# Heads of an attention: five of eight high parts on ScalarE, and scaling and splitting of sums in instructions of 1024 columns

## The chip, the cores and the metric

The kernel runs on one core of one Trainium2 chip. The time is device microseconds of one execution, the median of three runs where runs are compared, and one further execution carries the profile. The core's engines are TensorE (PE), VectorE (DVE), ScalarE (ACT), GpSimd (POOL) and SyncE (SP); a DMA is issued from the queue of SP or POOL here.

## The reference, cut

Six layers follow one another, each added to x of 4 x 1024 x 128 after a layer norm: experts, the attention of heads, experts, a recurrent layer, a second attention, a recurrent layer. The change is in the attention of heads alone:

```python
def _L0_attn_ref(x, weight):
    b, t, c = x.shape                 # 4, 1024, 128
    nh = NUM_HEADS                    # 16
    hs = c // nh                      # 8
    y = x.reshape(b, t, nh, hs).transpose(0, 2, 1, 3)
    scores = jnp.einsum('bhtk,bhsk->bhts', y, y) / math.sqrt(hs)
    attn = jax.nn.softmax(scores, axis=-1)
    o = jnp.einsum('bhts,bsc->bhtc', attn, x)
    o = o.transpose(0, 2, 1, 3).reshape(b, t, nh * c)
    return o @ weight
```

So there are 64 heads (4 batches of 16), each with scores of 1024 x 1024, a softmax over them, a product with the batch's 1024 x 128 values, and a product with 128 rows of the weight.

## The kernel before, in words

The function `head_attention` walks over 64 heads one after another. A head's scores are cut in eight tiles of 128 x 1024. Scores are symmetric but for the softmax's division, so the exponentials' row sums are kept apart and the division is done later, on the sums over the values: `scale` holds the inverse sums, spread over the partitions by a trip through DRAM.

A float32 product is made of three products of a reduced type (fp32r): each operand is split in a high part, which is a copy into fp32r, and a low part, which is the operand less its high part (`product`, lines 88 to 90). The steps for tile s of head h, whose running number is n = 8h + s:

- PE, `scores` (line 783): tiles s and s + 1 together, for even s, once the exponentials of all earlier tiles are done; two pairs of PSUM banks.
- ACT (line 835): the exponential of the tile out of PSUM into one of four buffers `e`, with the row sums; it waits for the scores and for the low part of tile n - 4.
- High part `e_hi`: on ACT (line 842) for the tiles in `ACT_HIGH`, directly behind that tile's exponential; on DVE (line 893) for the others.
- DVE (line 895): low part `e_lo`, which waits for the high part; DVE takes the tiles in order.
- PE, `weighted_rows`: the product of the tile with the values, six matmuls of 512 columns (two halves of 1024), six tiles behind the scores.

Once per head come the steps on its sums, here called u. DVE `scale_sums(h - 1)` (line 861) stands behind the low part of tile 5 of head h: it multiplies the sums of head h - 1, in two PSUM banks, by `scale`. The two banks are taken over by `weighted_rows` of tile 0 of head h, which waits for the scaling, for each half apart. ACT `u_highs(h - 1)` (line 825) stands behind the copy of tile 7, DVE `u_lows(h - 1)` (line 867) behind the low part of tile 7. PE `add_head(h - 2)` stands in the step of tiles 6 and 7, ahead of `weighted_rows` of tiles 0 and 1, and multiplies u by the weight. After 16 heads DVE's `add_batch` adds the finished batch to x, behind the low part of tile 3.

The order on each engine is that of the program; semaphores tie the engines. The order on PE in the steps of two tiles is:

```python
                for n in range(0, COUNT * TILES + TRAIL, 2):
                    if n < COUNT * TILES:
                        scores(n // TILES, n % TILES)
                    if n >= TRAIL:
                        if n % TILES == TRAIL and n // TILES >= 2:
                            add_head(n // TILES - 2)
                        for m in (n - TRAIL, n - TRAIL + 1):
                            weighted_rows(m // TILES, m % TILES)
```

SP stores the inverse sums and loads `scale` and the right operand of the scores, POOL loads the left operand; both run up to two heads ahead.

Of the kernel before, what the change touches and what calls it, by code (L numbers as in the profile page):

```python
# [8 lines left out]
F32R = mybir.dt.float32r  # L9
# [7 lines left out]
P = 128  # L17
BATCH, T = 4, 1024
TOKENS = BATCH * T
BANK = 512  # L20
# [53 lines left out]
def f(ap):  # L74

    return ap.bitcast(F32)
# [587 lines left out]
def head_attention(nc, tag, psum, consts, dram, x):  # L664


    with ExitStack() as ctx:
# [20 lines left out]
        inverse = sb(f"{tag}_inverse", [P, 2, 32])  # L688
        inverse_rows = sb(f"{tag}_inverse_rows", [P, 2, 32])
        scale = sb(f"{tag}_scale", [P, 2, T])  # L690
        u = sb(f"{tag}_u", [P, HALVES, BANK])
        u_hi, u_lo = sb(f"{tag}_u_hi", [P, 2, HALVES, BANK], F32R), sb(f"{tag}_u_lo", [P, 2, HALVES, BANK], F32R)
        SCORES, OUT, SUM = 0, 4, 6

        left_loaded, right_loaded = ([sem(f"{side}_{parity}") for parity in ("even", "odd")] for side in ("left", "right"))
# [6 lines left out]
        out_done, scaled_ready, u_high, u_low = sem("out"), sem("scaled"), sem("u_high"), sem("u_low")  # L702
        sum_done, added = sem("sum_done"), sem("added")
        HEAD_LOADS = 8
        ACT_HIGH = (1, 3, 5, 7)
        TRAIL = 6
        COUNT = BATCH * HEADS
        VALUE_BANKS = TOKENS // BANK
# [23 lines left out]
        with nc.Block() as block:  # L732
            @block.sync
            def _(sp):
                load_head(sp, right, (0, 1), 0, right_loaded)
                load_head(sp, right, (0, 1), 1, right_loaded)
                for h in range(COUNT):
                    sp.wait_ge(inverse_ready, h + 1)
                    after(sp, scale_loaded[h % 2], 16 * (h // 2))
                    for b in range(P // 32):  # L740
                        sp.dma_start(inverse_dram[h % 2, :].rearrange("(s b i) -> b s i", b=P // 32, i=32)[b],
                                     inverse_rows[b * 32:b * 32 + TILES, h % 2, :]).then_inc(inverse_stored, 16)
                    sp.wait_ge(inverse_stored, 16 * (P // 32) * (h + 1))
                    after(sp, scaled_ready, (h - 1) * HALVES)
                    sp.dma_start(scale[:, h % 2, :], inverse_dram[h % 2:h % 2 + 1, :].to_broadcast([P, T])
                                 ).then_inc(scale_loaded[h % 2], 16)
                    if h + 2 < COUNT:
                        sp.wait_ge(scores_done, (h + 1) * TILES)
                        load_head(sp, right, (0, 1), h + 2, right_loaded)
# [9 lines left out]
            @block.tensor  # L759
            def _(pe):  # L760
                def add_head(g):

                    cols = slice(g % HEADS * P, (g % HEADS + 1) * P)
                    pe.wait_ge(u_low, (g + 1) * HALVES)
                    if g % HEADS == 0:
                        after(pe, added, g // HEADS * HALVES)
                    for half in range(HALVES):
                        last = product(pe, psum[:, SUM + half, :], (w_hi[:, cols], w_lo[:, cols]),
                                       (u_hi[:, g % 2, half, :], u_lo[:, g % 2, half, :]),
                                       first=g % HEADS == 0, last=g % HEADS == HEADS - 1)  # L770
                    last.then_inc(sum_done, 1)

                def scores(h, s):

                    if s == 0:
                        pe.wait_ge(left_loaded[h % 2], 16 * HEAD_LOADS * (h // 2 + 1))
                        pe.wait_ge(right_loaded[h % 2], 16 * HEAD_LOADS * (h // 2 + 1))
                    after(pe, exp_done, h * TILES + s)
                    for tile in (s, s + 1):
                        for half in range(HALVES):  # L780
                            g = 2 * (tile % 2) + half
                            rows = slice(32 * g, 32 * (g + 1))
                            last = pe.matmul(psum[:, SCORES + g, :], left[rows, h % 2, tile * P:(tile + 1) * P],  # L783
                                             right[rows, h % 2, half * BANK:(half + 1) * BANK], start=True, stop=True)
                        last.then_inc(scores_done, 1)

                def weighted_rows(h, s):
                    pe.wait_ge(low, h * TILES + s + 1)
                    at_v = slice(h // HEADS * T + s * P, h // HEADS * T + (s + 1) * P)
                    for half in range(HALVES):  # L790
                        at = slice(half * BANK, (half + 1) * BANK)
                        if s == 0:
                            after(pe, scaled_ready, (h - 1) * HALVES + half + 1)
                        last = product(pe, psum[:, OUT + half, :], (v_hi[:, at_v], v_lo[:, at_v]),
                                       (e_hi[:, s, at], e_lo[:, s, at]), first=s == 0, last=s == TILES - 1)
                    last.then_inc(out_done, 1)

                for k in range(2 * VALUE_BANKS):
                    if k >= 8:
                        pe.wait_ge((v_by_act, v_by_dve)[k % 2], (k - 8) // 2 + 1)  # L800
                    for q in range(BANK // P):
                        at = slice(k % VALUE_BANKS * BANK + q * P, k % VALUE_BANKS * BANK + (q + 1) * P)
                        last = pe.transpose(psum[:, k % 8, q * P:(q + 1) * P],
                                            f((row_hi, row_lo)[k // VALUE_BANKS][:, at]), consts["identity"])
                    last.then_inc(turned, 1)
                pe.wait_ge(v_by_act, VALUE_BANKS)
                pe.wait_ge(v_by_dve, VALUE_BANKS)
# [8 lines that stand above are left out]
                for g in (COUNT - 2, COUNT - 1):  # L816
                    add_head(g)

            @block.scalar
            def _(act):  # L820
                def u_highs(g):
                    after(act, sum_done, g - 1)
                    for half in range(HALVES):
                        act.wait_ge(scaled_ready, g * HALVES + half + 1)
                        act.copy(u_hi[:, g % 2, half, :], u[:, half, :]).then_inc(u_high, 1)

                for k in range(0, 2 * VALUE_BANKS, 2):
                    act.wait_ge(turned, k + 1)
                    act.copy(turned_value(k), psum[:, k % 8, :]).then_inc(v_by_act, 1)
                for n in range(COUNT * TILES):  # L830
                    h, s = n // TILES, n % TILES
                    act.wait_ge(scores_done, n + 1)
                    after(act, low, n - 3)
                    wide = psum[:, SCORES + 2 * (s % 2):SCORES + 2 * (s % 2) + 2, :].rearrange("p a b -> p (a b)")
                    act.activation(e[:, s % 4, :], wide, ACT.Exp, scale=HEAD ** -0.5,  # L835
                                   accum_out=sums[:, h % 2, s:s + 1]).then_inc(exp_done, 1)
                    if s in ACT_HIGH:
                        act.wait_ge(exp_done, n + 1)
                        after(act, out_done, n - (TILES - 1))
                        if n < BATCH:  # L840
                            act.wait_ge(copied[n], BATCH_COPIED)
                        act.copy(e_hi[:, s, :], e[:, s % 4, :]).then_inc(act_high, 1)  # L842
                    if s == TILES - 1 and h >= 1:
                        u_highs(h - 1)
                u_highs(COUNT - 1)

            @block.vector
            def _(dve):
# [7 lines left out]
                def scale_sums(g):  # L856
                    dve.wait_ge(scale_loaded[g % 2], 16 * (g // 2 + 1))
                    dve.wait_ge(out_done, (g + 1) * TILES)
                    for half in range(HALVES):
                        after(dve, u_low, (g - 1) * HALVES + half + 1)  # L860
                        dve.tensor_tensor(u[:, half, :], scale[:, g % 2, half * BANK:(half + 1) * BANK],  # L861
                                          psum[:, OUT + half, :], ALU.mult).then_inc(scaled_ready, 1)

                def u_lows(g):
                    for half in range(HALVES):
                        dve.wait_ge(u_high, g * HALVES + half + 1)
                        dve.tensor_tensor(u_lo[:, g % 2, half, :], u[:, half, :], f(u_hi[:, g % 2, half, :]),
                                          ALU.subtract).then_inc(u_low, 1)

                def add_batch(b):  # L870
                    dve.wait_ge(sum_done, (b + 1) * HEADS)
# [864 lines left out]
```

## Time and profile before

| what | us |
|---|---|
| median of three runs (2739.37 to 2742.69) | 2742.0 |
| the profiled execution's own time | 2743.51 |
| its span, first to last instruction | 2741.4 |
| PE busy (93% of the span) | 2545.0 |
| DVE busy (81%) | 2223.1 |
| ACT busy (66%) | 1821.2 |
| POOL busy (45%) | 1231.3 |

All times in the rows are in microseconds from the span's start, except means of one instruction, in nanoseconds. The heads' first scaling stands at 682.5 and their last at 1657.5. In the timeline a row with x2 or x4 is a run of that many instructions and its length is from the first start to the last end; successive instructions of an engine overlap a little, so steps are best read from start to start. A bracket behind a row is the engine's idle time ahead of it and the instruction that released it. PE's matmuls are pipelined: they are shown 0.39 long, but follow one another after 0.23 at full clock.

### The profile page before, as it was taken

The numbers are of one execution on the slowest core, as the hardware profiler recorded it, in microseconds if no ns is written. First come the engines' busy times: TensorE is split into PE (matmuls) and PEld (weight loads), VectorE is DVE, ScalarE is ACT, GpSimd is POOL, SyncE is SP. The second block draws the span as 40 slices with busy tenths as digits, with TensorE's granted clock in tenths as the row PEclk, the third lists the DMA queues.
The fourth block names the chain that finished last, engine by engine and source line by source line (L and its number), as shares of the span: only waits on it lengthen the run. The fifth ranks groups of instructions, "written<-read, shape, count | busy, mean of one in ns | idle before, by whom it ended". The sixth has DMA issues, their size and how long they took to land. (4 is left out here: it accounts for less than half of the span.)

```text
span 2741.4 us, 35099 instructions
## 1 busy us (share of the span) xinstructions
PE 2545.0 (93%) x11075; PEld 1905.2 (69%) x11075; DVE 2223.1 (81%) x3277; ACT 1821.2 (66%) x3026; POOL 1231.3 (45%) x1265
## 2 busy tenths in 40 slices
PE   6899999996999999999999997899999998788778
PEld 3688888874666666666666664688888885476556
DVE  6778777776999999999999996777787775567655
ACT  3455555556888888888888884455555555557665
POOL 3466666664323232332323322466666662245401
PEclk9999999998999999999999999999999999888999
DMA  3566666644333333333333321566666640100000
GB/s 85 118 138 145 145 142 135 136 103 164 98 107 99 106 102 97 109 100 104 104 103 101 98 93 34 127 144 138 135 146 145 143 105 8 32 16 8 8 8 31
DMA packets 107385, 271.47 MB, mean 99 GB/s; under 512 B 30784, under 2 KB 35648, under 8 KB 107072
## 3 DMA queue, kind: packets, MB, share of 16 engines
q1 hardware_dynamic: 82192, 235.42, 34.7%
q0 software_dynamic: 24576, 33.62, 4.4%
q8 instruction: 88, 1.44, 0.2%
q14 instruction: 97, 0.79, 0.1%
q10 hardware_dynamic: 432, 0.20, 0.0%
HBM read 258.35 MB, written 10.76 MB: 98 GB/s over the span
## 5 line engine op out<-in xcount | busy, mean ns | idle before, releaser
L614 POOL TENSOR_TENSOR moe_experts_lo<-moe_experts_hidden,moe_experts_hi 128x512 fp32r<-128x512 f32 x512 | 661.1, 1291 | 340.6 <-ACT moe_experts_hi L552 340.4
L895 DVE TENSOR_TENSOR heads_e_lo<-heads_e,heads_e_hi 128x1024 fp32r<-128x1024 f32 x512 | 616.1, 1224 | 25.7
L559 ACT ACTIVATE psum<-psum 128x512 f32<-128x512 f32 x512 | 298.0, 582 | 479.8 <-PE psum L90 479.8
L729 POOL DMA_DIRECT2D heads_left<-heads_parts x512 | 306.5, 612 | 671.3 <-PE psum L783 610.7
L835 ACT ACTIVATE heads_e<-psum 128x1024 f32<-128x1024 f32 x512 | 520.0, 1023 | 108.2 <-PE psum L783 108.2
L586 DVE TENSOR_TENSOR moe_experts_weighted<-moe_spread,psum 128x512 f32<-128x512 f32 x512 | 350.8, 685 | 190.2 <-PE psum L90 186.4
L88 PE MATMUL psum<-heads_e_hi,heads_v_lo 128*128 128x512 f32 x1024 | 429.4, 419 | 18.0 <-DVE heads_u L861 18.0
L88 PE MATMUL psum<-moe_n_hi,moe_w_lo 128*128 128x512 f32 x1024 | 400.8, 391 | 4.2 <-PEq L54 3.9
L89 PE MATMUL psum<-heads_e_lo,heads_v_hi 128*128 128x512 f32 x1024 | 404.2, 395 | 0.0
L90 PE MATMUL psum<-heads_e_hi,heads_v_hi 128*128 128x512 f32 x1024 | 400.9, 391 | 0.0
L89 PE MATMUL psum<-moe_n_lo,moe_w_hi 128*128 128x512 f32 x1024 | 400.2, 391 | 0.0
L90 PE MATMUL psum<-moe_n_hi,moe_w_hi 128*128 128x512 f32 x1024 | 399.8, 390 | 0.0
L591 DVE TENSOR_TENSOR moe_experts_hidden<-moe_experts_weighted,psum 128x512 f32<-128x512 f32 x512 | 351.9, 687 | 34.4 <-POOL moe_experts_lo L614 17.7
L552 ACT CAST moe_experts_hi<-moe_experts_hidden 128x512 fp32r<-128x512 f32 x512 | 313.4, 612 | 1.3 <-DVE moe_experts_hidden L591 1.3
L88 PEld LDWEIGHTS psum<-heads_e_hi,heads_v_lo 128*128 128x128 f32 x1024 | 192.6, 188 | 124.3 <-issue 67.7
L842 ACT CAST heads_e_hi<-heads_e 128x1024 fp32r<-128x1024 f32 x256 | 269.3, 1052 | 8.1
L88 PEld LDWEIGHTS psum<-moe_n_hi,moe_w_lo 128*128 128x128 f32 x1024 | 193.3, 189 | 46.7 <-POOLq L624 5.4
L90 PEld LDWEIGHTS psum<-heads_e_hi,heads_v_hi 128*128 128x128 f32 x1024 | 193.2, 189 | 45.3
L90 PEld LDWEIGHTS psum<-moe_n_hi,moe_w_hi 128*128 128x128 f32 x1024 | 193.3, 189 | 40.5
L89 PEld LDWEIGHTS psum<-moe_n_lo,moe_w_hi 128*128 128x128 f32 x1024 | 193.4, 189 | 40.0
L89 PEld LDWEIGHTS psum<-heads_e_lo,heads_v_hi 128*128 128x128 f32 x1024 | 193.2, 189 | 32.3
L88 PE MATMUL psum<-moe_experts_hi,moe_w_lo 128*128 128x512 f32 x512 | 199.8, 390 | 2.4 <-POOL moe_experts_lo L614 2.4
(403 smaller groups left out, 4093.8 us busy)
## 6 DMA issues: line engine op xcount, KB each, us to landing
moe_spread<-moe_mask SPq DMA_DIRECT2D x128, 1024.0 KB, 9.8
heads_right<-heads_parts SPq DMA_DIRECT2D x512, 64.0 KB
heads_left<-heads_parts POOLq DMA_DIRECT2D x512, 64.0 KB, 2.5
heads_scale<-heads_inverse_copy SPq DMA_DIRECT2D x64, 512.0 KB, 3.7
moe_experts_raw<-in_gate SPq DMA_DIRECT2D x16, 256.0 KB, 11.7
moe_experts_raw<-in_up SPq DMA_DIRECT2D x16, 256.0 KB, 11.8
moe_experts_raw<-in_down SPq DMA_DIRECT2D x16, 256.0 KB, 11.6
heads_parts<-heads_e_hi SPq DMA_DIRECT2D x16, 256.0 KB, 3.2
```

What stands on the lines that cost most here:

```text
L88: pe.matmul(out, w_lo, x_hi, start=first, stop=False, skip_group_check=True)
L89: pe.matmul(out, w_hi, x_lo, start=False, stop=False, skip_group_check=True)
L90: return pe.matmul(out, w_hi, x_hi, start=False, stop=last, skip_group_check=True)
L552: act.copy(hi[:, p, :], hidden[:, p % 2, :]).then_inc(high_ready, 1)
L559: act.activation(psum[:, GATE + p % 2, :], psum[:, GATE + p % 2, :], ACT.Silu).then_inc(silu_ready, 1)
L586: dve.tensor_tensor(weighted[:, p % 2, :], spread[:, pair % 2, p, j * BANK:(j + 1) * BANK], psum[:, UP + p % 2, :], ALU.mult).then_inc(wei ...
L591: dve.tensor_tensor(hidden[:, p % 2, :], weighted[:, p % 2, :], psum[:, GATE + p % 2, :], ALU.mult).then_inc(hidden_ready, 1)
L614: pool.tensor_tensor(lo[:, p, :], hidden[:, p % 2, :], f(hi[:, p, :]), ALU.subtract).then_inc(low_ready, 1)
L729: eng.dma_start(f(tile[row:row + 2 * HEAD, h % 2, :]), parts_dram[dims, order:order + 2, at]).then_inc(loaded[h % 2], 16)
L835: act.activation(e[:, s % 4, :], wide, ACT.Exp, scale=HEAD ** -0.5, accum_out=sums[:, h % 2, s:s + 1]).then_inc(exp_done, 1)
L842: act.copy(e_hi[:, s, :], e[:, s % 4, :]).then_inc(act_high, 1)
L895: dve.tensor_tensor(e_lo[:, s, :], e[:, s % 4, :], f(e_hi[:, s, :]), ALU.subtract).then_inc(low, 1)
```

## The change

Tile 4 joins the tiles whose high part ACT makes, so ACT makes five and DVE three. The sums are held as 1024 columns in one piece: the scaling on DVE, the high part on ACT and the low part on DVE are one instruction of 1024 columns each, where they were two of 512. The semaphores of these steps count heads and no longer halves, so PE waits for the whole scaling ahead of both halves of `weighted_rows` of tile 0.

```diff
-        u = sb(f"{tag}_u", [P, HALVES, BANK])
-        u_hi, u_lo = sb(f"{tag}_u_hi", [P, 2, HALVES, BANK], F32R), sb(f"{tag}_u_lo", [P, 2, HALVES, BANK], F32R)
+        u = sb(f"{tag}_u", [P, T])
+        u_hi, u_lo = sb(f"{tag}_u_hi", [P, 2, T], F32R), sb(f"{tag}_u_lo", [P, 2, T], F32R)
...
-        ACT_HIGH = (1, 3, 5, 7)
+        ACT_HIGH = (1, 3, 4, 5, 7)
...
-                    after(sp, scaled_ready, (h - 1) * HALVES)
+                    after(sp, scaled_ready, h - 1)
...
-                    pe.wait_ge(u_low, (g + 1) * HALVES)
+                    pe.wait_ge(u_low, g + 1)
...
-                            after(pe, scaled_ready, (h - 1) * HALVES + half + 1)
+                            after(pe, scaled_ready, h)
...
                     after(act, sum_done, g - 1)
-                    for half in range(HALVES):
-                        act.wait_ge(scaled_ready, g * HALVES + half + 1)
-                        act.copy(u_hi[:, g % 2, half, :], u[:, half, :]).then_inc(u_high, 1)
+                    act.wait_ge(scaled_ready, g + 1)
+                    act.copy(u_hi[:, g % 2, :], u[:, :]).then_inc(u_high, 1)
...
-                    for half in range(HALVES):
-                        after(dve, u_low, (g - 1) * HALVES + half + 1)
-                        dve.tensor_tensor(u[:, half, :], scale[:, g % 2, half * BANK:(half + 1) * BANK],
-                                          psum[:, OUT + half, :], ALU.mult).then_inc(scaled_ready, 1)
+                    after(dve, u_low, g)
+                    dve.tensor_tensor(u[:, :], scale[:, g % 2, :], psum[:, OUT:OUT + 2, :].rearrange("p a b -> p (a b)"),
+                                      ALU.mult).then_inc(scaled_ready, 1)
 
                 def u_lows(g):
-                    for half in range(HALVES):
-                        dve.wait_ge(u_high, g * HALVES + half + 1)
-                        dve.tensor_tensor(u_lo[:, g % 2, half, :], u[:, half, :], f(u_hi[:, g % 2, half, :]),
-                                          ALU.subtract).then_inc(u_low, 1)
+                    dve.wait_ge(u_high, g + 1)
+                    dve.tensor_tensor(u_lo[:, g % 2, :], u[:, :], f(u_hi[:, g % 2, :]), ALU.subtract).then_inc(u_low, 1)
```

The order of ACT's instructions in one head of the steady part, from behind the high sums of one head to those of the next, before (x2 is two exponentials in a row):

```order
L825 CAST heads_u_hi<-heads_u 128x512 x2
L835 ACTIVATE heads_e,heads_sums<-psum 128x1024 x2
L842 CAST heads_e_hi<-heads_e 128x1024
L835 ACTIVATE heads_e,heads_sums<-psum 128x1024 x2
L842 CAST heads_e_hi<-heads_e 128x1024
L835 ACTIVATE heads_e,heads_sums<-psum 128x1024 x2
L842 CAST heads_e_hi<-heads_e 128x1024
L835 ACTIVATE heads_e,heads_sums<-psum 128x1024 x2
L842 CAST heads_e_hi<-heads_e 128x1024
```

and ACT's same head after the change:

```order
L825 CAST heads_u_hi<-heads_u 128x1024
L835 ACTIVATE heads_e,heads_sums<-psum 128x1024 x2
L842 CAST heads_e_hi<-heads_e 128x1024
L835 ACTIVATE heads_e,heads_sums<-psum 128x1024 x2
L842 CAST heads_e_hi<-heads_e 128x1024
L835 ACTIVATE heads_e,heads_sums<-psum 128x1024
L842 CAST heads_e_hi<-heads_e 128x1024
L835 ACTIVATE heads_e,heads_sums<-psum 128x1024
L842 CAST heads_e_hi<-heads_e 128x1024
L835 ACTIVATE heads_e,heads_sums<-psum 128x1024 x2
L842 CAST heads_e_hi<-heads_e 128x1024
```

The copy of tile 4 now stands between the exponentials of tiles 4 and 5. On DVE the same head, from behind the transposed inverse sums to the low part of the sums, before:

```order
L893 CAST heads_e_hi<-heads_e 128x1024
L895 TENSOR_TENSOR heads_e_lo<-heads_e,heads_e_hi 128x1024 x2
L893 CAST heads_e_hi<-heads_e 128x1024
L895 TENSOR_TENSOR heads_e_lo<-heads_e,heads_e_hi 128x1024 x2
L893 CAST heads_e_hi<-heads_e 128x1024
L895 TENSOR_TENSOR heads_e_lo<-heads_e,heads_e_hi 128x1024 x2
L861 TENSOR_TENSOR heads_u<-heads_scale,psum 128x512 x2
L893 CAST heads_e_hi<-heads_e 128x1024
L895 TENSOR_TENSOR heads_e_lo<-heads_e,heads_e_hi 128x1024 x2
```

and after the change (line numbers of the changed kernel):

```order
L890 CAST heads_e_hi<-heads_e 128x1024
L892 TENSOR_TENSOR heads_e_lo<-heads_e,heads_e_hi 128x1024 x2
L890 CAST heads_e_hi<-heads_e 128x1024
L892 TENSOR_TENSOR heads_e_lo<-heads_e,heads_e_hi 128x1024 x4
L860 TENSOR_TENSOR heads_u<-heads_scale,psum 128x1024
L890 CAST heads_e_hi<-heads_e 128x1024
L892 TENSOR_TENSOR heads_e_lo<-heads_e,heads_e_hi 128x1024 x2
```

DVE's copy of tile 4 is gone, so the low parts of tiles 2 to 5 stand in a row, and the scaling behind them is one instruction. PE's, SP's and POOL's instructions keep their order.

## Rows read from the trace of the kernel before

**Rows 1.** Windows: busy us (instructions) of each engine, granted PE clock, DMA share, GB/s.
```profile
720.00:1600.00 880.00, 864.95 (x3975) 596.53 (x3974) 849.49 (x1029) 779.62 (x1252) 271.03 (x452) 1.00 0.34 103
...
683.60:687.00 3.40, 3.40 (x9) 2.65 (x8) 3.37 (x5) 2.12 (x4) 3.05 (x5) 0.51 0.38 104
```
**Rows 2.** Timeline of PE, one head: start, length, line, operation [idle before <-releaser].
```profile
1112.82 0.50 PE L783 MATMUL psum<-heads_right,heads_left 32*128 32x512 f32 x4
...
1117.95 0.40 PE L90 MATMUL psum<-heads_u_hi,heads_w_hi 128*128 128x512 f32 x1
1118.56 0.47 PE L88 MATMUL psum<-heads_e_hi,heads_v_lo 128*128 128x512 f32 x1 [0.22 <-DVE heads_u L861]
...
1128.30 0.50 PE L783 MATMUL psum<-heads_right,heads_left 32*128 32x512 f32 x4
```
**Rows 3.** Timeline of ACT, the same head.
```profile
1113.36 1.03 ACT L835 ACTIVATE heads_e<-psum 128x1024 f32<-128x1024 f32 x1 [0.19 <-PE psum L783]
...
1114.37 1.02 ACT L835 ACTIVATE heads_e<-psum 128x1024 f32<-128x1024 f32 x1
...
1115.51 1.05 ACT L842 CAST heads_e_hi<-heads_e 128x1024 fp32r<-128x1024 f32 x1
...
1118.93 1.05 ACT L842 CAST heads_e_hi<-heads_e 128x1024 fp32r<-128x1024 f32 x1
1119.89 1.13 ACT L825 CAST heads_u_hi<-heads_u 128x512 fp32r<-128x512 f32 x2
```
**Rows 4.** Timeline of DVE, the same head.
```profile
1114.51 0.69 DVE L893 CAST heads_e_hi<-heads_e 128x1024 fp32r<-128x1024 f32 x1
1115.23 1.23 DVE L895 TENSOR_TENSOR heads_e_lo<-heads_e,heads_e_hi 128x1024 fp32r<-128x1024 f32 x1
1116.59 1.23 DVE L895 TENSOR_TENSOR heads_e_lo<-heads_e,heads_e_hi 128x1024 fp32r<-128x1024 f32 x1
1117.73 0.68 DVE L861 TENSOR_TENSOR heads_u<-heads_scale,psum 128x512 f32<-128x512 f32 x1
...
1118.93 0.69 DVE L893 CAST heads_e_hi<-heads_e 128x1024 fp32r<-128x1024 f32 x1
```
**Rows 5.** The scaling's line 861: who waited for it (us in all, times).
```profile
  PE psum L88: 18.0, 63
```
**Rows 6.** Groups by line and shape, 680 to 1660: busy us, mean ns | idle before.
```profile
L895 DVE TENSOR_TENSOR heads_e_lo<-heads_e,heads_e_hi 128x1024 fp32r<-128x1024 f32 x500 | 601.4, 1224 | 25.1
...
L867 DVE TENSOR_TENSOR heads_u_lo<-heads_u,heads_u_hi 128x512 fp32r<-128x512 f32 x128 | 82.3, 684 | 0.1
```
**Rows 7.** Timeline of DVE, a head in which a finished batch is added.
```profile
931.38 1.28 DVE L861 TENSOR_TENSOR heads_u<-heads_scale,psum 128x512 f32<-128x512 f32 x2
...
943.45 1.28 DVE L874 TENSOR_TENSOR x<-x,psum 128x512 f32<-128x512 f32 x2
...
947.65 1.28 DVE L861 TENSOR_TENSOR heads_u<-heads_scale,psum 128x512 f32<-128x512 f32 x2
```
**Rows 8.** Timelines of PE and DVE, from the first head to the second.
```profile
682.47 1.28 DVE L861 TENSOR_TENSOR heads_u<-heads_scale,psum 128x512 f32<-128x512 f32 x2
...
683.30 0.55 PE L88 MATMUL psum<-heads_e_hi,heads_v_lo 128*128 128x512 f32 x1 [1.81 <-DVE heads_u L861]
683.64 0.63 PE L89 MATMUL psum<-heads_e_lo,heads_v_hi 128*128 128x512 f32 x1
684.07 0.63 PE L90 MATMUL psum<-heads_e_hi,heads_v_hi 128*128 128x512 f32 x1
...
699.49 1.28 DVE L861 TENSOR_TENSOR heads_u<-heads_scale,psum 128x512 f32<-128x512 f32 x2
```
**Rows 9.** Timeline behind the last head.
```profile
1656.94 1.28 DVE L861 TENSOR_TENSOR heads_u<-heads_scale,psum 128x512 f32<-128x512 f32 x2 [6.22 <-PE psum L90]
...
1659.71 0.51 PE L88 MATMUL psum<-heads_u_hi,heads_w_lo 128*128 128x512 f32 x1 [1.48 <-DVE heads_u_lo L867]
```
**Rows 10.** The page's DMA issues: KB each, us to landing.
```profile
heads_scale<-heads_inverse_copy SPq DMA_DIRECT2D x64, 512.0 KB, 3.7
```

More of the change, by code:

```diff
@@ L767, in add_head @@
                     for half in range(HALVES):
+                        at = slice(half * BANK, (half + 1) * BANK)
                         last = product(pe, psum[:, SUM + half, :], (w_hi[:, cols], w_lo[:, cols]),
-                                       (u_hi[:, g % 2, half, :], u_lo[:, g % 2, half, :]),
+                                       (u_hi[:, g % 2, at], u_lo[:, g % 2, at]),
                                        first=g % HEADS == 0, last=g % HEADS == HEADS - 1)
```

## The prediction

> **What bounds the kernel now.** I read the windows by stage first [rows 1]. The change touches only the heads of the first attention, some 980 of 2741 us. In its steady part (720 to 1600 us) PE is busy 864.95 of 880 us, VectorE (DVE) 849.49 and ScalarE (ACT) 779.62, PE at a granted clock of 1.00. Three engines near full say nothing of which one sets the pace, so I followed one head by its start times.
>
> Second view, the timeline of PE, ACT and DVE over one head [rows 2 to 4]. I write exp, hi, low for what is done to a tile 0 to 7 of a head; "scale" for the scaling of the previous head's sums; "weighted 0" for the first product of a head with the values. Each arrow is a true dependence, by order on an engine or by a semaphore:
> - PE scores of tiles 4, 5 at 1112.82 -> exp 4 at 1113.36: 0.54
> - exp 4 -> exp 5 at 1114.37: 1.01
> - exp 5 -> hi 5 at 1115.51: 1.14
> - hi 5 -> DVE low 5 at 1116.59: 1.08 (it waits for that copy)
> - low 5 -> scale, first half, at 1117.73: 1.14 (DVE's order)
> - scale -> PE weighted 0 at 1118.56: 0.83, of which the instruction 0.68 and the hand-over 0.15
> - weighted 0 -> scores of tiles 4, 5 of the next head at 1128.30: 9.74 of PE's own work.
>
> Together 15.48, one head. The loop closes on itself, so it sets the pace. Two rows show it is tight: ACT sits idle 0.19 before exp 4, released by PE's scores [rows 3], and PE waits for the scale at nearly every head, 18.0 us in 63 times [rows 5]. PE bounds three quarters of the loop; the rest is a chain through ACT and DVE. Everything that lengthens that chain lengthens each head.
>
> **The change part by part.** Five against four high parts on ACT, the fifth being tile 4. DVE loses its copy of tile 4: 1114.51 to 1115.23, 0.72 per head [rows 4]. But that copy isn't in the loop: before low 5, DVE already waits for hi 5. So the saving is worth nothing there. ACT gains a copy between exp 4 and exp 5, which is in the loop. By ACT's rows, exp to its copy takes 1.14 (exp 5 -> hi 5), and a copy lets ACT's next instruction start after 0.96 (1118.93 -> 1119.89) [rows 3]; exp 4 -> exp 5 was 1.01. So exp 5, hi 5, low 5 and the scale come 1.14 + 0.96 - 1.01 = **1.09 us later**. A copy followed at once by an exp doesn't show in these rows: now each exp that follows a copy has waited for PE. Bounds: the copy's slot is 0.96 if the exp overlaps its end as another copy does, and 1.05 + 0.03 = 1.08 if it doesn't, so the term is 1.09 to 1.21, never below nothing, since it is an added instruction in ACT's order. I take 1.09, the row of the same copy.
>
> Scaling in one instruction of 1024. PE's weighted 0 needs the first 512 columns only, and did start after them. Now both of its halves wait for the whole. No row has a 1024 product out of PSUM. The 512 one takes 0.68 out of PSUM and 0.684 out of SBUF [rows 4, 6], and 1024 out of SBUF takes 1.224 [rows 6]: so 0.68 + 0.54 = 1.22. Bounds: 1.14, the spacing of two subtractions of 1024, and 1.28, 0.68 + 0.60 where two halves run as now. Term: 1.22 - 0.68 = **0.54 us later** per head (0.46 to 0.60). DVE's own saving, 1.20 for two halves (1117.73 to 1118.93) against 1.14, is 0.06 and not in the loop.
>
> The high and low parts in one instruction each. On ACT 1.13 for two become 1.05; on DVE 1.20 become 1.14. They run after tile 7 and are needed on PE a head later, so they cost and save nothing on the path. The scale's DMA lands a median 3.7 us after issue [rows 10]; it is issued at the head's start and is no nearer. The SP wait on the scaling counts heads in place of halves and still names a scaling two heads back; nothing moves there. POOL's loads are released by PE's scores, and follow the pace.
>
> Who is late next: with exp 5 at 2.64 after the scores (0.54 + 1.14 + 0.96), its end and accumulator at 3.75 hold PE's scores of tiles 6, 7, due at 3.42, for 0.4; then add_head runs on PE, ending at about 5.7; the scale runs from 6.0 to 7.2; weighted 0 starts at 7.4. So those 0.4 are hidden in a longer wait. ACT is through with its high sums at about 8.9 and PE's next scores come at 10.3, so ACT doesn't bound the loop otherwise. New loop: 15.48 + 1.09 + 0.54 = **17.11** per head, +1.63.
>
> Sum. 64 heads have 63 crossings: 63 x 1.63 = 102.7. Three heads also add a finished batch on DVE ahead of tile 4; one took 931.38 to 947.65 = 16.27 [rows 7], 0.79 over the loop's 15.48. That add lies beside the new ACT copy then: -2.4. After the last head the chain scale, high, low to the final add_head took 1656.94 to 1659.71 = 2.77 with halves overlapping [rows 9]; with whole tiles 1.22 + 1.05 + 1.22 and about 0.18 of hand-overs = 3.67: +0.9. Total **+101.2**. The profiled execution took 2743.5 us (span 2741.4, 2.1 around it), so 2844.7; it is 1.5 over the median of 2742.0, so **2843** by the median. The term bounds add 63 x (0 to 0.12) and 63 x (-0.08 to 0.06): 2838 to 2855.
>
> **The rivals.** First, faster. If DVE's occupancy set the pace, 0.72 + 0.06 + 0.06 = 0.84 per head would come free; PE would then stop it when its wait for the scale is gone: 18.0 us in all [rows 5], 2724. It decides if hi 4 fits into ACT's idle time, so that exp 5 isn't later. For it: DVE is 96.5% busy and ACT idles 100 of 880 us [rows 1]. Against it: the idle time lies ahead of exp 4, not between exp 4 and hi 5, and can't be used early, since PE's scores release it [rows 3]. The Trainium skill, Perfetto Trace Analysis, Optimizing Scalar/DVE Operations, says that larger operations help a saturated engine, and that a saturated DVE may hand work to Scalar. The same section says that where the two aren't saturated and leave bubbles on others, breaking instructions up may complete work sooner. By its first rule the time would be that of this rival; by its second the change goes the wrong way, and PE's wait for the scale is a bubble of that kind.
>
> Second, half of it: ACT's copy is hidden, and only the scale's 0.54 counts: 63 x 0.54 + 0.9, 2777. It decides from 1.1 us of slack before hi 5; the rows show none.
>
> Third, PE's clock. At the first crossing PE waited 1.81 for the scale at 683.30 and the next stretch ran at 0.51 of full clock, so mostly at 1.2 of 2.4 GHz, products 0.43 apart (683.64 to 684.07); that crossing took 682.47 to 699.49, 17.02, so 1.54 over the loop's 15.48 [rows 1, 8]. The new wait is nearly as long, about 1.6. If each head paid that: 63 x 1.54 = 97 on top, 2940; in a quarter of the heads, 2867. For it: the like wait. Against: at that crossing PE did no add_head between its scores and the wait, and all later heads do six products there. The Trainium skill, in Matmul Optimizations of the same page, says that TensorE's power scales with utilization and asks for back-to-back matmuls; by it this rival would be the likelier.
>
> **How the numbers follow.** Forecast 0.80, clock in some or all heads 0.10, scale alone 0.04, faster 0.05, nothing measurable 0.01. The likeliest is 2843, given as 2844 with the bounds leaning up. The range reaches below the term bounds, by some 12 us for spread in the rows, and upward to the clock in about a quarter to a third of the heads: 2826 to 2880. A measurement tells 0.2%, 5.5 us, from no change. Slower holds the forecast, the clock and the scale alone: 0.94; faster 0.05; same 0.01.
>
> **What would show it.** Right: scale starts 17.1 apart, the 1024 scale at 1.22, exp 4 to exp 5 at 2.1, PE's wait ahead of weighted 0 near 1.45 (about 90 us in all), and some 0.4 ahead of the scores of tile 6; DVE's and ACT's idle time up. Wrong: exp 5 not later than now after exp 4; DVE's low 5 starting before hi 5 would have ended; the period under 15.4; or products 0.43 apart inside the steady heads, which would be the clock.

## The result and the profile after

The changed kernel takes a median of 2849.9 us, the one before 2742.35: a ratio of 1.0395, 95% interval 1.0377 to 1.0413. It is slower by 3.95%; 2844 was forecast, with a range of 2826 to 2880. The profiled execution took 2851.95 us with a span of 2849.8.

The page of the kernel after, first the engines' busy time and share of the span, then two of the costliest groups (busy, mean ns, idle ahead of them and its releaser):

```profile
PE 2554.5 (90%) x11075; PEld 1910.6 (67%) x11075; DVE 2184.9 (77%) x3085; ACT 1876.1 (66%) x3026; POOL 1228.2 (43%) x1265
...
L892 DVE TENSOR_TENSOR heads_e_lo<-heads_e,heads_e_hi 128x1024 fp32r<-128x1024 f32 x512 | 622.0, 1225 | 150.8 <-ACT heads_e_hi L842 127.3
...
L88 PE MATMUL psum<-heads_e_hi,heads_v_lo 128*128 128x512 f32 x1024 | 429.5, 419 | 94.0 <-DVE heads_u L860 94.0
```

DVE's busy time fell by 38 us (2223.1 before) and ACT's rose by 55 (1821.2 before), the two ways that the change meant. What answers to [rows 5] is the last row: PE's wait for the scaling went from 18.0 to 94.0 us. And DVE, relieved, now idles 127.3 us ahead of low parts, released by ACT's copies; before, that group's 25.1 [rows 6] named nobody.

One head of the steady part, in the timeline of PE (to be read beside [rows 2]; the first column is the start):

```profile
1107.78 0.51 PE L784 MATMUL psum<-heads_right,heads_left 32*128 32x512 f32 x4
...
1110.85 0.39 PE L90 MATMUL psum<-heads_e_hi,heads_v_hi 128*128 128x512 f32 x1
1111.58 0.51 PE L784 MATMUL psum<-heads_right,heads_left 32*128 32x512 f32 x4 [0.34 <-ACT heads_e L835]
...
1113.29 0.39 PE L90 MATMUL psum<-heads_u_hi,heads_w_hi 128*128 128x512 f32 x1
1115.14 0.47 PE L88 MATMUL psum<-heads_e_hi,heads_v_lo 128*128 128x512 f32 x1 [1.46 <-DVE heads_u L860]
...
1124.86 0.51 PE L784 MATMUL psum<-heads_right,heads_left 32*128 32x512 f32 x4
```

of ACT (beside [rows 3]):

```profile
1108.32 1.03 ACT L835 ACTIVATE heads_e<-psum 128x1024 f32<-128x1024 f32 x1 [0.22 <-PE psum L784]
...
1109.46 1.05 ACT L842 CAST heads_e_hi<-heads_e 128x1024 fp32r<-128x1024 f32 x1
1110.42 1.02 ACT L835 ACTIVATE heads_e<-psum 128x1024 f32<-128x1024 f32 x1
...
1111.56 1.05 ACT L842 CAST heads_e_hi<-heads_e 128x1024 fp32r<-128x1024 f32 x1
```

and of DVE (beside [rows 4]):

```profile
1110.55 1.23 DVE L892 TENSOR_TENSOR heads_e_lo<-heads_e,heads_e_hi 128x1024 fp32r<-128x1024 f32 x1 [1.19 <-ACT heads_e_hi L842]
1112.64 1.23 DVE L892 TENSOR_TENSOR heads_e_lo<-heads_e,heads_e_hi 128x1024 fp32r<-128x1024 f32 x1 [0.86 <-ACT heads_e_hi L842]
1113.78 1.21 DVE L860 TENSOR_TENSOR heads_u<-heads_scale,psum 128x1024 f32<-128x1024 f32 x1
```

The reader can walk the loop by the starts: scores of tile 4 at 1107.78, exp 4 at 1108.32, its copy at 1109.46, exp 5 at 1110.42, its copy at 1111.56, low 5 at 1112.64, the scaling at 1113.78, PE's first product at 1115.14, the next head's scores of tile 4 at 1124.86. That is 17.08 us for a head that took 15.46 to 15.48. PE's wait ahead of that first product is 1.46, where it was 0.22 [rows 2], and the 0.34 ahead of the scores of tile 6 is new.

### The profile page after: what moved, and what is told of

Same layout as the page of the kernel before. It is cut to its first block and busy times, and to the rows that moved or that the text cites. A ratio compares the mean times of both kernels' runs of the same rounds, so it can differ in the third digit from the quotient of the medians.

```text
span 2849.8 us, 34907 instructions
## 1 busy us (share of the span) xinstructions
PE 2554.5 (90%) x11075; PEld 1910.6 (67%) x11075; DVE 2184.9 (77%) x3085; ACT 1876.1 (66%) x3026; POOL 1228.2 (43%) x1265
## 5 line engine op out<-in xcount | busy, mean ns | idle before, releaser
L892 DVE TENSOR_TENSOR heads_e_lo<-heads_e,heads_e_hi 128x1024 fp32r<-128x1024 f32 x512 | 622.0, 1225 | 150.8 <-ACT heads_e_hi L842 127.3
L591 DVE TENSOR_TENSOR moe_experts_hidden<-moe_experts_weighted,psum 128x512 f32<-128x512 f32 x512 | 351.9, 687 | 35.0 <-POOL moe_experts_lo L614 18.1
L842 ACT CAST heads_e_hi<-heads_e 128x1024 fp32r<-128x1024 f32 x320 | 336.0, 1050 | 10.1
```

The source lines that it names most:

```text
L591: dve.tensor_tensor(hidden[:, p % 2, :], weighted[:, p % 2, :], psum[:, GATE + p % 2, :], ALU.mult).then_inc(hidden_ready, 1)
L892: dve.tensor_tensor(e_lo[:, s, :], e[:, s % 4, :], f(e_hi[:, s, :]), ALU.subtract).then_inc(low, 1)
```

## The experiments

Each kernel was run beside the kernel before on the same chip. "Spacing" is from one scaling to the next in the steady heads of the profiled execution (the median); a passage from one scaling to the next is called a crossing.

| kernel | copies on ACT | sums | scaling behind | spacing us | PE's wait for scaling, us | median us | ratio, 95% interval |
|---|---|---|---|---|---|---|---|
| before | 1 3 5 7 | halves | low 5 | 15.46 | 18.0 | 2738.7 to 2742.4 | 1 |
| after | 1 3 4 5 7 | whole | low 5 | 17.08 | 94.0 | 2849.9 | 1.0377 to 1.0413 |
| e1_five_only | 1 3 4 5 7 | halves | low 5 | 16.53 | 60.5 | 2805.0 | 1.0217 to 1.0248 |
| e2_wide_only | 1 3 5 7 | whole | low 5 | 15.99 | 51.7 | 2775.8 | 1.0108 to 1.0142 |
| e3_tile6 | 1 3 5 6 7 | whole | low 5 | 15.99 | 51.8 | 2784.0 | 1.0131 to 1.0166 |
| e8_parts_wide | 1 3 5 7 | parts whole | low 5 | 15.46 | 18.1 | 2740.7 | 1.0001 to 1.0020 |
| e4_scale_early | 1 3 5 7 | halves | low 4 | 15.03 | 0.5 | 2709.8 | 0.9869 to 0.9899 |
| e9_scale_early_2 | 1 3 5 7 | halves | low 4 | 15.03 | 0.5 | 2707.2 | 0.9869 to 0.9902 |
| e7_wide_early | 1 3 5 7 | whole | low 4 | 15.03 | 2.3 | 2713.0 | 0.9880 to 0.9913 |
| e6_tile6_early | 1 3 5 6 7 | whole | low 4 | 15.03, some up to 16.39 | 3.3 | 2725.4 | 0.9928 to 0.9958 |
| e5_after_early | 1 3 4 5 7 | whole | low 4 | 15.37 | 1.0 | 2735.8 | 0.9971 to 0.9997 |

**Each part of the change alone.** First the fifth copy, in the kernel before:

```diff
-        ACT_HIGH = (1, 3, 5, 7)
+        ACT_HIGH = (1, 3, 4, 5, 7)
```

> The kernel before with one edit: ACT makes the high part of tile 4 too; scaling and both parts of the sums stay in halves of 512. Theory (the loop scores 4, exp 4, exp 5, hi 5, low 5, scale, weighted 0): the copy stands between exp 4 and exp 5 and adds 1.09 to each head, so heads go from 15.46 to 16.55 and the time to about 2742 + 63 x 1.09 - 2.4 = 2808. Rival (DVE's load sets the pace): DVE loses 0.72 per head, so the time falls towards PE's bound, 2724, or stays at 2742. Second rival (only the wider scaling costs): 2742.

Measured: 2805.0, heads of 16.53, so 1.07 each. Taking 0.72 of work off DVE made the kernel slower by 64 us. That is against both rivals. Then the sums' instructions of 1024 columns, in the kernel after:

```diff
-        ACT_HIGH = (1, 3, 4, 5, 7)
+        ACT_HIGH = (1, 3, 5, 7)
```

> The kernel after with four high parts on ACT as before: only the scaling and the two parts of the sums are in one instruction of 1024. Theory: PE's first product of a head waits for the whole scaling, 1.21 in place of 0.68, so 0.53 to 0.54 per head: heads of 16.00 and 2742 + 34 + 1 = 2777. Rival (DVE's load): one instruction fewer for each, 0.12 less per head on DVE, so 2735 to 2742. Together with the run that has five copies alone, the two additions should make the whole change if they lie in one chain: 66 + 35 = 101.

Measured: 2775.8 and 15.99. 1.07 and 0.53 make 1.60 of the 1.62 per head that the whole change has: the two lie one behind the other in a single chain. (The medians rose by 64 and 35, 99 together, where the whole change has 108; what is missing lies outside the steady heads, see the account below.) The scaling itself took what a 512 product plus the step of a subtraction gave; by its line in this kernel (duration in ns, minimum, median and maximum; and who waited):

```profile
L860 DVE TENSOR_TENSOR heads_u<-heads_scale,psum x64: 1210/1211/1221, 682.6 to 1691.1; 128x1024 f32<-128x1024 f32 x64
...
  PE psum L88: 51.7, 63
```

Which of the three wide instructions costs: the kernel with wide parts but the scaling in halves.

```diff
-                    dve.tensor_tensor(u[:, :], scale[:, g % 2, :], psum[:, OUT:OUT + 2, :].rearrange("p a b -> p (a b)"),
-                                      ALU.mult).then_inc(scaled_ready, 1)
+                    for half in range(HALVES):
+                        at = slice(half * BANK, (half + 1) * BANK)
+                        dve.tensor_tensor(u[:, at], scale[:, g % 2, at], psum[:, OUT + half, :],
+                                          ALU.mult).then_inc(scaled_ready, 1)
```

The diff is cut: ACT also makes four copies again, and PE, ACT and SP count the halves of the scaling again, so PE waits for each half apart.

> Of the change only the high and the low part of the sums in one instruction of 1024 columns each: four copies on ACT, the scaling in halves of 512, for each of which PE waits apart. Theory: what the wide form cost was the scaling alone (0.53 per head), and the parts run behind tile 7, off the loop, so heads take 15.46 as before and the time is 2741, +1 for the tail. Rival (any of the three wide instructions costs): part of the 0.53 shows here, 2750 or more.

Measured: 2740.7, heads of 15.46, PE's wait 18.1. All of the 0.53 is the wider scaling; in the steady heads the parts are free, in both directions. The median is 1.9 above that of the kernel before that ran beside it (2738.7), where 1 was expected for the tail.

**The same load in another place.** The fifth copy moved from tile 4 to tile 6, in the kernel after:

```diff
-        ACT_HIGH = (1, 3, 4, 5, 7)
+        ACT_HIGH = (1, 3, 5, 6, 7)
```

> The kernel after with another fifth tile: ACT makes the high part of tile 6 in place of tile 4. ACT's and DVE's work per head is the same as in the kernel after, to the instruction; only its place differs. Theory: exp 6, hi 6, exp 7 lie behind hi 5 and in the time in which PE waits for the scaling, so this copy costs nothing and only the wider scaling is left: heads of 16.00, 2777, as with four copies. Rival (ACT's load of five copies and the wide sums set the pace): as the kernel after, 17.08 per head and 2850.

Measured: heads of 15.99, to the hundredth those of the kernel with four copies. Five copies on ACT cost nothing here, with the same instructions on both engines as the kernel after. In ACT's timeline the copy of tile 6 stands between the two exponentials, and the next head's first exponential still finds ACT idle, waiting for PE:

```profile
1309.14 1.03 ACT L835 ACTIVATE heads_e<-psum 128x1024 f32<-128x1024 f32 x1 [0.21 <-PE psum L784]
...
1310.29 1.05 ACT L842 CAST heads_e_hi<-heads_e 128x1024 fp32r<-128x1024 f32 x1
1311.24 1.02 ACT L835 ACTIVATE heads_e<-psum 128x1024 f32<-128x1024 f32 x1
...
1312.39 1.05 ACT L842 CAST heads_e_hi<-heads_e 128x1024 fp32r<-128x1024 f32 x1
1313.34 1.05 ACT L825 CAST heads_u_hi<-heads_u 128x1024 fp32r<-128x1024 f32 x1
1314.91 1.03 ACT L835 ACTIVATE heads_e<-psum 128x1024 f32<-128x1024 f32 x1 [0.52 <-PE psum L784]
```

The median, 2784.0, is 7 over the 2777 expected; the heads don't have it, and one of the four executions took 2775.66 (see the late layers below).

**The loop cut open.** No work changes; the scaling goes one place up in DVE's order, in the kernel before:

```diff
-                    if s == TRAIL - 1 and h >= 1:
+                    if s == TRAIL - 2 and h >= 1:
                         scale_sums(h - 1)
```

> The kernel before with the scaling of the last head's sums one place earlier in DVE's order, behind the low part of tile 4 and ahead of that of tile 5. No work changes. Theory: hi 5 and low 5 leave the loop; the scaling is then released by the last product of the head before, so PE's wait for it, 18.0 in 63 heads, goes: heads of 15.17, 2742 - 18 = 2724, unless DVE (at least 14.9 per head) is next and gives less, up to 2735. Rival (the pace is a load of DVE, ACT or PE): the same loads give the same 2742.

Measured: 2709.8, 31 us under the kernel before, heads of 15.03. The direction is the theory's, the gain is larger than the 18 forecast. PE at the same place as in [rows 2], the last product of add_head and the first of the new head:

```profile
1101.96 0.39 PE L90 MATMUL psum<-heads_u_hi,heads_w_hi 128*128 128x512 f32 x1
1102.19 0.40 PE L88 MATMUL psum<-heads_e_hi,heads_v_lo 128*128 128x512 f32 x1
```

They start 0.23 apart, where they were 0.61 apart [rows 2]. So the wait had cost 0.38 a head and not the 0.22 in its bracket: the bracket counts from the shown end of a matmul, 0.39 behind its start, though the next could start after 0.23. 63 x 0.38 = 24; a further 0.05 per head came from a source that wasn't traced, and the first crossing took 14.73 in place of 17.02 [rows 8], another 2. In the stage from 720 to 1600 us PE is now busy 879.50 of 880 us, so 15.03 is the length of PE's own work. The same kernel once more:

> The kernel before with the scaling behind the low part of tile 4, once more with more rounds, for the interval of the version that beats both kernels. Theory: heads of 15.03, 2708 to 2712. Rival (the first look was lucky in the late layers, whose length differs by some us between executions): up to 2718.

Measured: 2707.2, interval 0.9869 to 0.9902. This is the version that beats both kernels; it is 1.15% below the kernel before.

**The change with the loop cut open.** The same move of the scaling in three kernels with the change or a part of it. Wide sums, four copies:

```diff
-        ACT_HIGH = (1, 3, 4, 5, 7)
+        ACT_HIGH = (1, 3, 5, 7)
...
-                    if s == TRAIL - 1 and h >= 1:
+                    if s == TRAIL - 2 and h >= 1:
```

> Four copies as before, the sums in one instruction of 1024 each, the scaling early. Theory: released by the last product of the head before, the scaling of 1024 ends some 0.5 ahead of PE's first product, so its width costs nothing any more: 15.03 per head, 2710. Rival (the wider instruction costs wherever it stands): 15.5 per head, 2743.

Measured: 15.03 and 2713.0. In the steady heads the wide scaling has no cost of its own; it had it by its place in the loop. What is left of it are four heads in which PE waited 2.3 us in all for it, where with halves (e4) one head waited 0.5. The kernel after with the early scaling alone:

```diff
-                    if s == TRAIL - 1 and h >= 1:
+                    if s == TRAIL - 2 and h >= 1:
```

> The kernel after with one edit: the scaling stands behind the low part of tile 4, ahead of that of tile 5. Theory: the copy of tile 4 on ACT is out of the loop through the scaling, but exp 5 still ends at 3.75 after the scores of tile 4, and PE is ready for the scores of tiles 6, 7 at 3.42, so a shorter loop through ACT alone (scores 4, exp 4, hi 4, exp 5, scores 6) takes its place: the 15.03 per head that the kernel before had with the early scaling, and 0.40 on top, 15.43, so about 2710 + 25 = 2735. Rival (the fifth copy costs only through the scaling): 15.03 and 2710. Second rival (loads): 2850, as the kernel after.

Measured: 15.37 per head and 2735.8, with 15.43 and 2735 expected. PE's scores in this kernel show what is left of 0.34 per head over the 15.03, the wait for exp 5 that lay hidden in the kernel after:

```profile
1306.24 0.51 PE L784 MATMUL psum<-heads_right,heads_left 32*128 32x512 f32 x4
1310.04 0.50 PE L784 MATMUL psum<-heads_right,heads_left 32*128 32x512 f32 x4 [0.35 <-ACT heads_e L835]
```

And tile 6 for the fifth copy with the early scaling, which has all of the change's instructions outside both loops:

```diff
-        ACT_HIGH = (1, 3, 4, 5, 7)
+        ACT_HIGH = (1, 3, 5, 6, 7)
...
-                    if s == TRAIL - 1 and h >= 1:
+                    if s == TRAIL - 2 and h >= 1:
```

> The kernel after with tile 6 in place of tile 4 and the scaling early: all of the change's instructions, in a place where neither loop has them. Theory: PE's own work is the bound, 15.03 per head, 2708 to 2712, no better than the early scaling with four copies and halves, since PE doesn't notice DVE's saved 0.84. Rival (DVE was the bound in that run, whose heads took 14.72 behind an added batch): 14.72 per head or less, 2690.

Measured: 2725.4, above both expectations. Most heads took the 15.02 to 15.04 of PE's own work, so DVE wasn't what held the early scaling with four copies, and DVE's saved time again bought nothing. But eighteen heads took 15.15 to 16.39, of which three add a batch (16.21 to 16.23; in e4 such a head takes 16.04), and four times PE waited for a head's first scores. Around the worst, SP's queue and PE:

```profile
1248.98 1.30 SPq L741 DMA_DIRECT2D heads_inverse_copy<-heads_inverse_rows  x4
1251.16 0.35 SPq L745 DMA_DIRECT2D heads_scale<-heads_inverse_copy  x1
...
1264.01 1.29 SPq L741 DMA_DIRECT2D heads_inverse_copy<-heads_inverse_rows  x4
1268.00 0.35 SPq L745 DMA_DIRECT2D heads_scale<-heads_inverse_copy  x1
1268.39 5.58 SPq L729 DMA_DIRECT2D heads_right<-heads_parts  x8
...
1277.81 0.51 PE L784 MATMUL psum<-heads_right,heads_left 32*128 32x512 f32 x4 [1.51 <-issue]
```

There the inverse sums' store took 3.99 from issue to the load behind it, where the head before had 2.18, and the loads of the scores' right operand, queued behind on SP, ran as much later. That this delay is what PE waited for is read from the order of the rows; it wasn't tried by itself, and why such stores came oftener in this kernel than in e4 (15.38 and 15.55 in two heads) is open. From the first scaling to the last this kernel took 952.1 us and e4 944.6, so the heads account for 7.6 of the 13 us between their spans; 3.3 more arose in the late layers (446.6 against 443.3).

## Why the prediction was right

The steps in its own order:

- **The loop.** Forecast 17.11 per head from 0.54, 1.14, 0.96, 1.14, 1.08, 1.14, 1.22 + 0.15 and 9.74. Measured 0.54, 1.14, 0.96, 1.14, 1.08, 1.14, 1.36 and 9.72: 17.08. A copy followed by an exponential has the 0.96 of a copy followed by a copy, at the lower of the two bounds. The prediction took this from a neighbouring pair and said that by now each exponential behind a copy has waited for PE. That holds for the steady heads only: in the first head of the same trace of before, an exponential follows a copy at once, 0.95 behind it, so the term could have been read:

```profile
659.14 1.05 ACT L842 CAST heads_e_hi<-heads_e 128x1024 fp32r<-128x1024 f32 x1
660.09 1.02 ACT L835 ACTIVATE heads_e<-psum 128x1024 f32<-128x1024 f32 x1
```

- **The fifth copy.** 1.09 forecast; 1.07 alone.
- **The wide scaling.** 0.54 forecast; 0.53 alone, and none from the two parts.
- **DVE's saved work** was priced at nothing. e3 and e6 bear that out: the same saving in another place made no head shorter.
- **Who is late next.** The scores of tile 6 were to wait 0.4: 1110.85 to 1111.58 is 0.73 from start to start, where 0.32 is usual, so 0.41, hidden in the kernel after. e5 brought it to light, with 15.37 per head in place of 15.03.
- **PE's wait**, near 1.45 a head and 90 in all: 1.46 and 94.0. By starts it is 1113.29 to 1115.14, 1.85, so 1.62 over the usual 0.23; this is the 1.6 that the clock's rival names.
- **Added batches.** The heads with an added batch no longer stand out (all steady heads 17.06 to 17.11), as the -2.4 had it.

The rivals fell. DVE's load as the pace: e1 took DVE's load down and lost 64 us; e4 left every load as it was and won 31. The Trainium skill says in Perfetto Trace Analysis, Optimizing Scalar/DVE Operations, that breaking up instructions may let work complete sooner where Scalar and Vector aren't saturated but cause bubbles on other engines. The scaling in halves fits this where PE waits for it: 0.53 per head sooner behind low 5 (e2), nothing behind low 4 (e7). The clock as a rival: the half clock came at the first crossing as it did before (18.51, so 1.43 over the loop, with products 0.43 apart from 687.10 on), but in the steady heads of the kernel after the granted clock is 1.00:

```profile
720.00:1700.00 980.00, 875.24 (x4012) 602.25 (x4012) 826.69 (x868) 835.41 (x1261) 274.97 (x463) 1.00 0.31 93
```

Two terms were missing. The sum of +101.2 compares with +108.4 in the spans. Up to the first gates of the first recurrent layer, behind the heads and the second layer of experts, the kernel after is 103.6 late (2401.58 against 2297.97), so the sum is short by 2.4 there. From the first scaling to the last the kernel after took 98.8 more, where the crossings and the batches were forecast at 100.3: the last crossing grew by 0.55 only, from 12.06 to 12.61. Behind the last scaling another 2.1 came: the 0.9 of the tail as forecast (1758.46 to 1762.13, so 3.67), and 1.2 in code that doesn't change, which wasn't traced. And the first scaling already came 2.7 later (685.17 against 682.47), which the sum with its 63 crossings left out. The way from the heads' first scores to that scaling shows where: it took 26.0 us before (from 656.45) and 29.1 after (from 656.09), 27.9 in e1_five_only and 26.1 in e2_wide_only. So the fifth copy made 1.9 of the 3.1; tile 4 of two heads lies on that way. The other 1.2 go with a lower granted clock of PE, which from 10 to 20 us behind the first scores was 0.68 in the kernel after and 0.81 in e1_five_only; whether the change brought that about wasn't tried.

The other 4.8 arose behind that point, in code that the change doesn't touch, and the prediction had no term for it. The windows from there to the end, for before, after and e7_wide_early (busy time of PE, weight loads, DVE, ACT, POOL; granted clock; DMA):

```profile
2297.97:2741.37 443.40, 359.16 (x1454) 271.44 (x1452) 281.46 (x345) 277.55 (x431) 126.31 (x107) 0.88 0.05 16
```

```profile
2401.58:2849.78 448.20, 366.10 (x1454) 277.04 (x1452) 280.01 (x345) 277.61 (x431) 126.33 (x107) 0.87 0.05 16
```

```profile
2268.20:2706.17 437.97, 353.31 (x1454) 264.82 (x1452) 282.32 (x345) 277.26 (x431) 124.45 (x107) 0.90 0.05 16
```

The same instructions take 438 to 448 us, the longer the lower PE's granted clock; e3_tile6 has 448.27 at 0.87, e6_tile6_early 446.61 at 0.87, e1_five_only 443.35 at 0.89. In these six the length goes with the clock. It doesn't go with the change: e1 has the fifth copy in tile 4 and the length of before, e3 has it elsewhere and the length of after. It covers most of e3's 7 us too. Executions of one and the same kernel differ too: e4 and e9 are one kernel, with 443.3 and 440.0 here, and the ten executions of e5_after_early run from 2729.05 to 2742.61, the five shortest at a granted clock of 0.965 to 0.968 over the whole execution and the five longest at 0.964 (in which layers, these times don't tell). The four of the kernel after, though, lie within 3.2, so whether a later start of these layers shifts their clock too is open.

The early scaling's gain, forecast at 18 in the experiment and in the faster rival's bound, was 31: what failed there is the reading of PE's wait from its bracket, above.

## What to carry to other kernels

Where several engines are near full, find the loop that closes on itself from one iteration to the next and price each edit by whether it lies in it: the same copy cost 1.07 us in tile 4 and nothing in tile 6, and the same wide instruction cost 0.53 behind low 5 and nothing behind low 4. Taking work off a nearly full engine by putting it on another one's path between a producer and its consumer makes the loop longer. The cheapest gain was in the order: an instruction that others wait for stands ahead of one that itself has to wait.

## What was not expected of the hardware

A wait of PE reads too short where it follows a matmul: 0.22 in the bracket was 0.38 from start to start, since the matmul ahead is shown 0.39 long and in e4 the next started 0.23 behind it.

One wait's length alone doesn't tell whether PE's clock falls. The kernel before waited 1.81 at its first crossing and ran the next stretch at 0.51 [rows 1, 8]; e1_five_only waited 2.52 at the same crossing and stayed at full clock, 1.00 over the same window:

```profile
684.04 0.47 PE L88 MATMUL psum<-heads_e_hi,heads_v_lo 128*128 128x512 f32 x1 [2.52 <-DVE heads_u L861]
```

```profile
683.60:687.00 3.40, 2.96 (x16) 2.20 (x16) 3.37 (x5) 2.55 (x5) 2.70 (x5) 1.00 0.41 116
```

Its head took 16.57 there, where the kernel before took 17.02, although its loop is longer. Neither kernel has products of add_head ahead of that crossing's wait, so the lack of these products, by which the prediction set the first crossing apart, doesn't by itself bring the clock down.
